# Moving the small adapter weight chain into the prologue steps, and whole-tile DMAs in place of pairs of halves

## What is computed

```python
xn = layernorm(x)
r = sigmoid(xn @ Wr.T); k = xn @ Wk.T; v = xn @ Wv.T
dec = sigmoid(decay); log_decay = log(clip(dec, 1e-7))
scale = exp(t * log_decay)
state = cumsum(k * v / clip(scale, 1e-10), axis=time) * scale
x = x + rmsnorm(r * state, ln_w) @ Wo.T

lilora = up_aux @ (lora_up @ (lora_down @ down_aux))
x = x + layernorm(x) @ W.T + b + layernorm(x) @ lilora.T
```

## Time and profile before

| | us |
|---|---|
| two timed runs | 866.09 and 892.53 |
| their median | 879.31 |
| profiled execution | 864.17 |
| its span (slowest core, core 3) | 862.4 |
| spans of the 8 cores | 856.9 to 862.4 |

### The profile page before, as it was taken

The page is one execution under the profiler, slowest core; times in us unless marked ns, Lnnn a source line. Parts: engine busy times, 40 slices in busy tenths (PEclk is TensorE's granted clock), DMA queues, the critical chain, the costliest instruction groups (busy, mean ns, idle before and its releaser), DMA issues.

```text
span 862.4 us, 9105 instructions; the slowest of 8 cores (856.9 to 862.4 us)
## 1 busy us (share of the span) xinstructions
PE 526.9 (61%) x2558; PEld 248.1 (29%) x2558; DVE 359.5 (42%) x478; ACT 335.7 (39%) x452; POOL 77.7 (9%) x43
## 2 busy tenths in 40 slices
PE   1343420799445468552463985577777664999994
PEld 1232310343122223221231432233333321444441
DVE  3334420144422334334423462454454432667664
ACT  3566550333333333344344441534434412223322
POOL 1000000122310003201110211111111100000000
PEclk9999999999877779766876997688988866999998
DMA  6899811300011110021000000421112103354443
GB/s 136 197 212 214 195 28 18 81 1 1 0 49 49 49 49 1 1 49 32 17 25 1 1 0 1 97 50 49 49 50 49 49 0 98 98 145 112 135 139 82
DMA packets 21187, 56.31 MB, mean 65 GB/s; under 512 B 7598, under 2 KB 7598, under 8 KB 21138
## 3 DMA queue, kind: packets, MB, share of 16 engines
q1 hardware_dynamic: 21138, 55.73, 26.4%
HBM read 47.32 MB, written 8.39 MB: 65 GB/s over the span
## 4 chain that ended last, share of the span: by engine, by line
PE 40%; DVE 20%; ACT 16%; issue 9%; POOL 5%; DMA 5%; SPq 1%; DVEq 1%; ACTq 0%; POOLq 0%
PE psK L405 13%; PE psV L405 8%; PE psV L632 4%; PE psTb L286 4%; POOL k_m L446 3%; PE psR L683 3%; ACT lnT L393 2%; PE psK L683 2%; PE psTb L388 2%; DVE u_m L516 2%; ACT slotA L294 2%; DVE u_m L484 2%; POOL k_m L510 2%; DVE u_m L426 2%; ACT csbuf L504 2%
## 5 line engine op out<-in xcount | busy, mean ns | idle before, releaser
L405 PE MATMUL psK<-lnT,slotA 128*128 128x512 bf16 x512 | 150.4, 459 | 6.5 <-ACT lnT L393 6.5
L405 PE MATMUL psV<-lnT,slotB 128*128 128x512 bf16 x512 | 115.7, 379 | 3.6 <-DVE u_m L426 3.6
L405 PEld LDWEIGHTS psK<-lnT,slotA 128*128 128x128 bf16 x512 | 58.8, 117 | 90.1 <-issue 53.4
L388 PE MATMUL psTb<-ident_t,yA 128*128 128x128 bf16 x192 | 22.7, 292 | 76.9 <-ACT lnT L393 46.9
L405 PEld LDWEIGHTS psV<-lnT,slotB 128*128 128x128 bf16 x512 | 49.7, 98 | 65.4 <-issue 6.4
L286 PE MATMUL psTb<-ident_t,castbuf 128*128 128x128 bf16 x224 | 25.5, 285 | 66.5 <-DVE castbuf L280 37.8
L446 POOL TENSOR_TENSOR k_m<-u_m,csbuf 128x1024 f32<-128x1024 f32 x16 | 37.6, 2352 | 307.6 <-ACT csbuf L442 307.6
L510 POOL TENSOR_TENSOR k_m<-u_m,csbuf 128x1024 f32<-128x1024 f32 x16 | 37.5, 2341 | 303.6 <-ACT csbuf L504 303.6
L405 PE MATMUL psR<-lnT,slotC 128*128 128x512 bf16 x256 | 59.5, 387 | 4.4 <-ACT csbuf L529 4.4
L632 PE MATMUL psV<-slotB,lnT 128*128 128x512 bf16 x256 | 59.3, 386 | 2.7 <-DVE u_m L655 1.4
L484 DVE TENSOR_TENSOR u_m<-k_m,psV 128x1024 f32<-128x1024 f32 x16 | 19.6, 1222 | 87.0 <-ACT csbuf L494 56.8
(11 more groups left out here) (134 smaller groups left out, 707.8 us busy)
## 6 DMA issues: line engine op xcount, KB each, us to landing
xt<-x_own SPq DMA_DIRECT2D x54, 256.0 KB, 4.0
xt<-x_pre SPq DMA_DIRECT2D x22, 256.0 KB, 5.9
wstage<-Wo SPq DMA_DIRECT2D x16, 256.0 KB, 3.8
xt<-Wf SPq DMA_DIRECT2D x16, 256.0 KB, 3.8
out<-k_m SPq DMA_DIRECT2D x12, 256.0 KB, 3.2
x1tc<-x_pre SPq DMA_DIRECT2D x10, 256.0 KB, 6.0
x1tc<-x_own SPq DMA_DIRECT2D x10, 256.0 KB, 4.0
out<-u_m SPq DMA_DIRECT2D x10, 256.0 KB, 3.1
```

The costliest lines, as they stand in the source:

```text
L388: return e.transpose(psTb[:, j * 128:(j + 1) * 128], lnc[:, j * 128:(j + 1) * 128], ident_t[:])
L405: return e.matmul(ps[:, j * 512:(j + 1) * 512], wtile(slot, kc, m), lnT_mt(kc, h * H + j * 512, 512), start=(kc == 0), stop=(kc == 7))
```

## The change

Two things. First, the halves become whole: every load and store of 128 rows is one DMA of 512 KB, with one semaphore, and the waits on the second semaphores go. Second, the adapter chain is cut into twelve functions (`lsteps`): lora_down, lora_up, eight up_aux chunks, down_aux with m1, and m2. One is emitted at the end of each prologue step from s = 3 to 14, behind the weight rounds of that step. They use x1t1 and castbuf2 in place of wstage and castbuf. The `apply_ve` variant of `ln_chunk_p1`, which nothing calls, goes too.

```diff
             @E("sync", xs, inc_n=16,
-               waits=[last_applyx[slot], ("ve", last_bnx[slot])])
+               waits=[("sc", last_applyx[slot]), ("ve", last_bnx[slot])])
             def _(e, i=i, xt=xt):
-                return e.dma_start(out=xt[0:64, :],
-                                   in_=src_h[i * 128:i * 128 + 64, :])
-            @E("sync", xs + "b", inc_n=16,
-               waits=[last_applyx[slot], ("ve", last_bnx[slot])])
-            def _(e, i=i, xt=xt):
-                return e.dma_start(out=xt[64:128, :],
-                                   in_=src_h[i * 128 + 64:(i + 1) * 128, :])
+                return e.dma_start(out=xt[:], in_=src_h[i * 128:(i + 1) * 128, :])
...
+        lsteps = []
+
+        def _l_ld():
+            @E("sync", "ld", inc_n=16, waits=[("ld", c("ld"))])
+            def _(e): return e.dma_start(out=x1t1[0:4, 0:100], in_=ld_h)
+            @E("vector", "ve", waits=[("ld", c("ld"))])
+            def _(e): return e.tensor_copy(castbuf2[0:4, 0:100], x1t1[0:4, 0:100])
+            @E("tensor", "mm", waits=[("ve", c("ve")), ("sc", psTbg["sc"])])
+            def _(e): return e.transpose(psTb[0:100, 0:4], castbuf2[0:4, 0:100],
+                                         ident_t[0:4, 0:4])
+            @E("scalar", "sc", waits=[("mm", c("mm"))])
+            def _(e): return e.copy(out=ldT[:], in_=psTb[0:100, 0:4])
+            psTbg["sc"] = c("sc")
+        lsteps.append(_l_ld)
+
+        def _l_lu():
+            @E("sync", "ld", inc_n=16, waits=[("ve", c("ve")), ("ld", c("ld"))])
+            def _(e): return e.dma_start(out=x1t1[0:50, 0:4], in_=lu_h)
+            @E("vector", "ve", waits=[("ld", c("ld")), ("mm", c("mm"))])
...
+        def _l_ua(rc):
+            @E("sync", "ld", inc_n=16, waits=[("ve", c("ve")), ("sc", c("sc")),
+                                              ("ld", c("ld"))])
+            def _(e, rc=rc):
+                return e.dma_start(out=x1t1[:, 0:50],
+                                   in_=ua_h[rc * 128:(rc + 1) * 128, :])
+            @E("vector", "ve", waits=[("ld", c("ld")), ("mm", c("mm"))])
+            def _(e): return e.tensor_copy(castbuf2[:, 0:50], x1t1[:, 0:50])
+            @E("tensor", "mm", waits=[("ve", c("ve")), ("sc", psTbg["sc"])])
+            def _(e): return e.transpose(psTb[0:50, 0:128], castbuf2[:, 0:50],
+                                         ident_t[:])
+            @E("scalar", "sc", waits=[("mm", c("mm"))])
+            def _(e, rc=rc):
+                return e.copy(out=uaT[:, rc * 128:(rc + 1) * 128],
+                              in_=psTb[0:50, 0:128])
+            psTbg["sc"] = c("sc")
+        for _rc in range(8):
+            lsteps.append(lambda rc=_rc: _l_ua(rc))
+
+        def _l_m1():
+            @E("sync", "ld", inc_n=16, waits=[("ve", c("ve")), ("ld", c("ld"))])
+            def _(e): return e.dma_start(out=x1t1[0:100, :], in_=da_h)
+            @E("vector", "ve", waits=[("ld", c("ld")), ("sc", c("sc")),
+                                      ("mm", c("mm"))])
+            def _(e): return e.tensor_copy(castbuf2[0:100, :], x1t1[0:100, :])
...
+        def _l_m2():
+            for j in range(2):
+                @E("tensor", "mm", waits=[("sc", c("sc"))])
...
         lnq = []
         for s in range(16):
             lnq.append(ln_chunk_p1(x_pre, s))
             if len(lnq) == 2:
                 ln_chunk_p2(lnq.pop(0), rdy_pre)
             for _ in range(2):
                 if ri < len(rounds):
                     srch, slot, rc = rounds[ri]
                     slot_done[id(slot)] = weight_round(
                         srch, slot, rc, stages_pro[ri % 2], cbufs_pro[ri % 2])
                     ri += 1
+            if s >= 3 and lsteps:
+                lsteps.pop(0)()
...
-        @E("sync", "ld", inc_n=16,
-           waits=[("ve", wstate["cast"].get(id(wstage), 0)),
-                  ("ld", c("ld")), ("w0", c("w0")), ("w1", c("w1"))])
-        def _(e): return e.dma_start(out=wstage[0:4, 0:100], in_=ld_h)
...
+        while lsteps:
+            lsteps.pop(0)()
```

More of the change, by code:

```diff
@@ L247, in _ @@
             def _(e, rc=rc, stage=stage):
[L248 to L254, removed]
+                return e.dma_start(out=stage[:],
+                                   in_=src_h[rc * 128:(rc + 1) * 128, :])
             ldv = c(ws)
-            ldvb = c(ws + "b")
             if m3_ps is not None:
@@ L259, in _ @@
                     @E("tensor", "mm",
-                       waits=(([(ws, ldv), (ws + "b", ldvb), ("sc", c("sc"))]
-                               + list(m3_w))
+                       waits=(([(ws, ldv), ("sc", c("sc"))] + list(m3_w))
                               if j == 0 else ()))
@@ L267, in _ @@
                                         start=True, stop=True)
-                @E("vector", "ve", waits=[("mm", c("mm")), (ws, ldv),
-                                          (ws + "b", ldvb)])
+                @E("vector", "ve", waits=[("mm", c("mm")), (ws, ldv)])
                 def _(e, stage=stage, m3_ps=m3_ps):
@@ L306, in weight_round @@
             return c("sc")
[L308 removed]
+        last_apply = {0: 0, 1: 0}
         last_bn = {0: 0, 1: 0}
@@ L363, in ln_chunk_p1, with _ @@
             ve_negmi = c("ve")
[L364 to L378, removed]
+            @E("scalar", "sc", waits=[("ve", ve_negmi), ("mm", last_tp[par])])
+            def _(e, xt=xt, cols=cols, lnc=lnc):
+                return e.activation(out=lnc, in_=xt[:], func=AF.Identity,
+                                    bias=cols[:, 2:3], scale=cols[:, 1:2])
+            last_apply[par] = last_applyx[slot] = sc_apply = c("sc")
             return dict(i=i, par=par, lnc=lnc, sc_apply=sc_apply)
@@ L384, in _ @@
                 @E("tensor", "mm",
-                   waits=([ctx["sc_apply"], ("sc", psTbg["sc"])]
+                   waits=([("sc", max(ctx["sc_apply"], psTbg["sc"]))]
                           if j == 0 else ()))
@@ L649, in stageC @@
                 st_l1["oa"] = c("ve")
-                sts = "st" + str(ig % 3)
-                @E("vector", "ve", waits=[(sts, oring_st[ig % 3][0]),
-                                          (sts + "b", oring_st[ig % 3][1]),
+                @E("vector", "ve", waits=[("st" + str(ig % 3), oring_st[ig % 3]),
                                           ("ld", ld_b), ("gp", gp_all)])
@@ L656, in stageC @@
                 last_x1[par] = ve_out = c("ve")
+                sts = "st" + str(ig % 3)
                 @E("sync", sts, inc_n=16, waits=[("ve", ve_out)])
                 def _(e, ig=ig, ot=ot):
[L659 to L665, removed]
+                    return e.dma_start(out=out_h[ig * 128:(ig + 1) * 128, :],
+                                       in_=ot[:])
+                oring_st[ig % 3] = c(sts)
             wo_mm = {}
@@ L718, in _ @@
                             return e.dma_start(
[L719 to L728, removed]
+                                out=xtp[:],
+                                in_=x_own[igp * 128:(igp + 1) * 128, :])
+                        ld_pre[igp] = (xsp, c(xsp))
                     ld_x = ld_pre[ig]
@@ new lines, in build_nc, with _ @@
+        lsteps.append(_l_ld)
[3 more added lines that the diff above has]
+            @E("vector", "ve", waits=[("ld", c("ld")), ("mm", c("mm"))])
+            def _(e): return e.tensor_copy(castbuf2[0:50, 0:4], x1t1[0:50, 0:4])
+            @E("tensor", "mm", waits=[("ve", c("ve")), ("sc", psTbg["sc"])])
+            def _(e): return e.transpose(psTb[0:4, 0:50], castbuf2[0:50, 0:4],
+                                         ident_t[0:50, 0:50])
+            @E("scalar", "sc", waits=[("mm", c("mm"))])
+            def _(e): return e.copy(out=luT[:], in_=psTb[0:4, 0:50])
+            psTbg["sc"] = c("sc")
@@ new lines, in build_nc @@
+        lsteps.append(_l_lu)
+        def _l_ua(rc):
[6 more added lines that the diff above has]
+            def _(e): return e.tensor_copy(castbuf2[:, 0:50], x1t1[:, 0:50])
+            @E("tensor", "mm", waits=[("ve", c("ve")), ("sc", psTbg["sc"])])
+            def _(e): return e.transpose(psTb[0:50, 0:128], castbuf2[:, 0:50],
+                                         ident_t[:])
+            @E("scalar", "sc", waits=[("mm", c("mm"))])
+            def _(e, rc=rc):
+                return e.copy(out=uaT[:, rc * 128:(rc + 1) * 128],
+                              in_=psTb[0:50, 0:128])
+            psTbg["sc"] = c("sc")
@@ new lines, in build_nc, with _ @@
+        for _rc in range(8):
[6 more added lines that the diff above has]
+            def _(e): return e.tensor_copy(castbuf2[0:100, :], x1t1[0:100, :])
+            ve_da = c("ve")
+            for j in range(2):
+                @E("tensor", "mm",
+                   waits=([("ve", ve_da), ("sc", c("sc"))] if j == 0 else ()))
+                def _(e, j=j):
+                    return e.matmul(psR[0:4, j * 512:(j + 1) * 512], ldT[:],
+                                    castbuf2[0:100, j * 512:(j + 1) * 512],
```

(54 more changed lines are left out.)

42 lines of the change are left out of this document (10 added, 32 removed).

## The result

| | before | after |
|---|---|---|
| median of the timed runs, us | 872.53 (10 runs) | 885.7 (11 runs) |
| lowest to highest, us | 865.99 to 892.53 | 884.33 to 893.38 |
| profiled execution, us | 864.17 | 887.0 |
| its span, us | 862.4 | 885.5 |
| first projection, median of the 8 cores, us | 154.3 | 180.2 |

A forecast was written before the change was run, and what follows sets the result against it. The prediction saw the adapter chain as exposed latency before the projections, and its moved loads as delaying each prologue step's x load: 864.2 + 37.4 (later first projection) - 1.4 (unsplit DMAs) = 900 us, range 884 to 920.

The forecast's parts named there:

- What goes (36.6 us): The lone adapter chain between the last normalised chunk's copy and the first projection goes entirely: 36.6 us.
- The block: Prologue: up_aux load waits for the step's end, holding x on SP's queue and bn_stats on DVE; cycle 15.3 against 7.56.
- E: End of a prologue step's second weight tile copy; the next x load was put at 0.6 us after it.
- step 3: Prologue step with lora_down: no blocking wait on SP, one more use of the single psTb, 0.6 us.
- step 5: Prologue step after lora_up: x issued at 49.8 instead of 42.60, landing at 54.7, step ending at 64.4.
- blocked steps: Prologue steps whose x load waits behind an up_aux load; steps 6 to 11 put at 15.3 us each, 91.8 in all.
- L: Landing time of a 512 KB x load in the prologue, from first issue: 4.9 us, with 4.3 to 5.9 for its own range.
- step 12: Prologue step without weights: 0.6 + 4.9 + 0.1 + 5.16 = 10.8 us, to 167.0.
- The unsplit DMAs (-1.4): Whole loads and stores, mostly after the first projection: fewer issues and semaphore waits, -1.4 us in all.
- A: Prologue: the small chain pieces slip between steps at 0.6 to 1 us each, total 837 us; chance 0.07.
- B: Prologue: only DVE's order binds, x is there in time, cycle 12.4 us, total 874 us; chance 0.08.
- C: Prologue: single large loads slower than pairs, landing in 5.9 to 7.1 us, total 909 to 920; chance 0.13.

The follow-up runs named there:

- e4: Changed kernel, but the chain's loads wait only for the cast of the chain's previous piece, not all of DVE and ACT: 850.59 us, 0.9758 of the kernel before.
- e1: Kernel before with whole DMAs alone, the adapter chain left behind the prologue: ratio 0.9979 to the kernel before.
- e5: As e4, and the chain's casts wait only for the chain's own last transpose, not all of PE: ratio 0.9747 to the kernel before.
- e3: Changed kernel with the next step's x load issued ahead of the chain's load: 876.32 us, ratio 1.0043 to the kernel before.
- e6: Kernel before with whole DMAs, chain loads issued in step 13 into own columns, its PE work between the first projections: 829.75 us, 0.9563 of the kernel before.
- e2: Kernel before with the chain moved into steps 3 to 14, DMAs still in halves: 907.91 us, ratio 1.0424 to the kernel before.

## Why the prediction was right or wrong

**What goes (36.6 us)**: right. The stretch is gone, and the first projection follows the last transposes.

**The block**: right in kind and in both of its parts. x is issued at E + 0.6 (121.48 to 122.08), the step from bn_stats on takes 9.67, the waits are where they were placed, and e4 removes the loss by the waits alone. The increments match term by term: step 3 plus 0.69 (0.6 forecast), step 5 10.41 (10.4), the first two blocked steps 15.31 and 15.32 (15.3), down_aux issued 3.0 after bn_stats (2.9), m2 2.3 (2.3). That is the profiled core, the slowest. On cores 0, 3, 4 and 7 step 5 took 9.1 to 9.3 us and the first blocked step 13.6 to 13.8, so the exact match of those two is in part luck of the core.

**The step that failed: L = 4.9 us for "a 512 KB load on an empty queue with a burst behind it"**, nine times in the sum. It was read from a pair of halves, with the second issue in it; the change issues whole loads, and these landed in 3.3 to 3.9 in six of the eight blocked steps (4.9 and 4.5 in the first two). Steps 8 to 11 came out at 14.7, 14.0, 13.8, 13.8: -4.9 us in all; step 12 -1.2, bn_stats of step 13 -1.3, x behind down_aux -1.5, the end -0.4. The first three, 7.4 us, are L. With 2.3 for the late start of core 3's trace, that is, within the rounding, the 11.5 us between the forecast +37.4 and the measured +25.9 (157.75 to 183.66). My lower bound for L, 4.3, was from a pair as well, so the late steps lay outside both ends. That the time is in the range all the same is owed to the 6 us that the range had below 890, which no term stood for. The Trainium skill's fit for GpSimd's queues (DMA: Bandwidth & Descriptors, Anatomy of one DMA), 2.0 us plus bytes over 436 GB/s, gives an estimate of 3.2 and with it a total of 885; I had set it aside because the rows were at 4.3. Measured landings of whole loads and stores on SP's queue come near it in part: 3.3 for the x load at 122.08, and for the stores from k_m and u_m a median of 2.9 on six of the eight cores, but 3.7 to 3.8 on cores 2 and 3, and 4.9 for the x load at 62.70. The rows didn't speak against it, since none of them was a single 128-row load.

**The unsplit DMAs (-1.4)**: right in sign, too small. From the first projection on, the median core takes 3.7 us less (704.9 to 701.2). On core 2 the last scan is 4.1 us nearer to the first projection (536.8 to 532.7), and the first store another 2.5 (581.3 to 574.7 in all), where I had 0 to 0.6 for the start of the final stage. e1 has the same (534.5 and 576.2). Some of it goes with the clock: before, cores 4 and 6, at 0.870 over the span, took 702.9 and 703.7 from the first projection on and the others 704.6 to 707.5, while in e1 the four cores at 0.869 or 0.870 took 699.5 to 702.9; at equal clock about 2 us are left. What gave them wasn't tried. Up to the first projection, whole loads are worth 12 us in the blocked steps (192.1 to 180.2), which I hadn't priced, having used the pair's number for both.

**Rivals.** A (hidden, 837, which is 27 us less) is near what the move does once its waits are its own: undisturbed cores end 22.3 us sooner in e4 and 32.6 in e5. For the changed kernel it is out. B (874) asked for x to be in time, and e3, which makes it so, runs at 870 (876 the median of the timed runs): the price was right, the condition wasn't met. C (slow single loads) is out, and its down_aux row misled: here the load of 100 rows took 5.4 us to its cast (165.86 to 171.28; 4.4 to 6.4 over the cores), while 128 rows took 3.5 to bn_stats (122.08 to 125.58). The rule that a load of 100 partitions is spread over 10 engines and one of 128 over 16 (the Trainium skill, DMA: Bandwidth & Descriptors, Why a DMA increments its semaphore by 16) has that direction. With the fit above it doesn't give the size: 400 KB at 10/16 of 436 GB/s comes to an estimate of 3.5 us. Other loads were issued behind each of the two, and no run here varied the rows alone, so the cause stays open.

## What to carry to other kernels

Before moving a serial chain into a pipelined loop, look at what its waits stand for: "everything emitted so far" costs little at a seam (SP waited 6.0 us in all for the copies of the lone chain), and in a loop it ties each step's prefetch to the end of the step before, through the DMA queue and through the order of each engine. Give each moved load and cast the wait for the last reader of its own buffer, or a buffer of its own, and move it then; here that is the difference between 2% slower and 2% faster (e4), or 4% where the loads have room of their own and are issued ahead, and the chain's PE work stands between the first projections (e6). And price a transfer from a row of the same form: a pair of halves is no measure of one whole load.

## What the runs showed of the hardware that was not expected

A 512 KB load as one DMA of 128 rows landed 3.3 us after its issue where a pair of 64-row halves needed 4.6 from the first issue (0.62 to the second, and 4.0 for it; e2, issued at 124.23 and 124.85), and whole stores from k_m landed in 2.9 on six cores (3.7 on cores 2 and 3) against 3.2 for the halves before. While the queue was kept full, in e1, this made no difference from step 3 on: steps of 7.56 us either way. In the first two blocked steps of the changed kernel, the first of which the eight cores reached within 2.8 us of each other (step 5 ended between 59.3 and 62.1), the same whole load took 4.9 and 4.5 us on the profiled core; in the late ones, with step 11 ending between 142.3 and 149.0, it took 3.3. The cores that reached the first blocked step earliest had the short landings (3.2 to 3.4) already there, the later four the long ones (4.7 to 5.4). That the cores' bursts collide at first and drift apart later would explain it, and was not tried.
